# One burst of four attention-value groups, a ring of six probability tiles, and a stack load that is issued one step later

## What is computed

```
xn = layernorm(x)
q, k, v = xn @ Wq.T + bq, xn @ Wk.T + bk, xn @ Wv.T + bv      # 16 heads of 8
attn = softmax(where(causal, q @ k.T / sqrt(8), -inf))
a = (attn @ v) @ Wo.T + bo
top_val, top_idx = top_k(xn @ gate_w.T, 2);  w = softmax(top_val)
f = sum over the two of (xn @ We[top_idx]) * w
out = x + a + f
```

## Time and profile before

| | |
|---|---|
| median of three runs | 515.52 us (513.57 to 517.12) |
| the profiled execution | 512.65 us |
| its span, from first to last instruction | 510.5 us |
| TensorE matmul busy | 94% of the span |
| VectorE, ScalarE, GpSimd busy | 82%, 78%, 68% |
| mean granted clock of TensorE | 0.998 |
| DMA queue of SyncE | 66.68 MB, 53% of 16 engines |

### The profile page before, as it was taken

How to read it: one execution, slowest core, us unless ns; L and a number is a source line. 1 busy time by engine, 2 the same in 40 slices (tenths; PEclk the granted TensorE clock), 3 DMA queues, 4 the chain that set the end, 5 groups by cost and what they waited for, 6 DMA issues and landing times.

```text
span 510.5 us, 17312 instructions
## 1 busy us (share of the span) xinstructions
PE 477.8 (94%) x6274; PEld 393.8 (77%) x6274; DVE 420.7 (82%) x1111; ACT 396.9 (78%) x1062; POOL 345.9 (68%) x561
## 2 busy tenths in 40 slices
PE   2548799999999999999999999999999999999995
PEld 1437688888888888888888888888888888888863
DVE  5897698888888898888888898888888898888721
ACT  3644688888888888888888888888888888887773
POOL 7264657777777777778777777777777777755443
PEclk9999999999999999999999999999999999999999
DMA  4664746656547566655465566655556566552000
GB/s 124 195 140 117 188 122 152 161 136 156 134 119 162 130 151 156 160 139 145 105 168 128 148 154 160 156 141 143 139 128 147 138 152 161 133 132 44 15 13 22
DMA packets 64281, 67.79 MB, mean 133 GB/s; under 512 B 6828, under 2 KB 59180, under 8 KB 59484
## 3 DMA queue, kind: packets, MB, share of 16 engines
q1 hardware_dynamic: 64196, 66.68, 53.0%
HBM read 44.90 MB, written 21.23 MB: 130 GB/s over the span
## 4 chain that ended last, share of the span: by engine, by line
PE 89%; DVE 3%; ACT 3%; DMA 2%; issue 2%; SPq 0%; POOL 0%; DVEq 0%; POOLq 0%; ACTq 0%
PE m L841 23%; PE oT_ps L911 17%; PE scoreT_ps L887 13%; PE score_ps L867 12%; PE scoreT_ps L892 5%; PE score_ps L861 5%; PE m L953 3%; PE m L996 3%; PE m L1014 3%; PE m L926 2%; PE m L1021 1%; PE m L962 1%; DMA qstack<-mT 1%; ACT probs L499 1%; DVE negmax L625 1%
## 5 line engine op out<-in xcount | busy, mean ns | idle before, releaser
L625 DVE TENSOR_REDUCE negmax<-score_ps 128x2 f32<-128x512 f32 (+1 forms) x384 | 249.7, 678 | 46.4 <-PE score_ps L867 43.7
L499 ACT ACTIVATE probs<-scoreT_ps 128x512 f32<-128x512 f32 x384 | 216.5, 603 | 74.2 <-PE scoreT_ps L887 48.0
L394 POOL TENSOR_TENSOR fours<-lower,upper 128x512 f32<-128x512 f32 x64 | 81.7, 1276 | 54.1 <-ACT upper L549 54.1
L841 PE MATMUL m<-we_hl,xnT_hl 128*128 128x512 f32 x384 | 114.6, 420 | 0.0
L867 PE MATMUL score_ps<-kstack,qstack 72*128 72x128 bf16 (+1 forms) x1024 | 103.8, 224 | 5.6 <-DVE negmax L625 5.5
L887 PE MATMUL scoreT_ps<-qstack,kstack 123*128 123x128 bf16 (+1 forms) x1024 | 102.0, 221 | 3.3 <-DMA qstack<-mT 2.6
L911 PE MATMUL oT_ps<-probs,vaug 128*32 128x256 f32 (+1 forms) x2048 | 96.7, 329 | 0.2 <-ACT probs L499 0.2
L887 PEld LDWEIGHTS scoreT_ps<-qstack,kstack 123*128 123x128 bf16 (+1 forms) x1024 | 68.1, 98 | 26.5 <-ACT probs L499 15.4
L911 PEld LDWEIGHTS oT_ps<-probs,vaug 128*32 128x32 f32 x2048 | 57.3, 109 | 29.1 <-ACT probs L499 0.4
L549 ACT ACTIVATE upper<-m,weight 128x128 f32<-128x128 f32 x256 | 73.1, 376 | 8.2 <-PE m L841 8.2
L867 PEld LDWEIGHTS score_ps<-kstack,qstack 72*128 72x128 bf16 (+1 forms) x1024 | 72.1, 100 | 8.8 <-DVE negmax L625 7.6
(11 more groups left out here) (81 smaller groups left out, 649.7 us busy)
## 6 DMA issues: line engine op xcount, KB each, us to landing
kstack<-scratch SPq DMA_DIRECT2D x93, 192.0 KB
scratch<-parts SPq DMA_DIRECT2D x64, 192.0 KB, 2.4
qstack<-scratch SPq DMA_DIRECT2D x62, 192.0 KB
qstack<-scratch SPq DMA_DIRECT2D x31, 256.0 KB
x_sb<-in_x SPq DMA_DIRECT2D x32, 128.0 KB, 2.3
scratch<-parts SPq DMA_DIRECT2D x32, 128.0 KB, 1.9
out<-out_sb SPq DMA_DIRECT2D x32, 128.0 KB, 3.7
qstack<-mT SPq DMA_DIRECT2D x64, 8.0 KB, 2.1
```

What stands on the lines that cost most here:

```text
L394: g.tensor_tensor(fours[:, :, q, :], lower[:, :, q, :], upper[:, :, q, :], ALU.add).then_inc(pool_sum, 1)
L499: a.activation(o, i, ACT.Exp, scale=SCALE).then_inc(act_exp, 1)
L625: v.tensor_reduce(o, score_ps[n % 2][:].rearrange("p (h k) -> p h k", h=w), axis=AX.X, op=ALU.max, negate=True).then_inc(dve_max, 1)
L841: ins = tn.matmul(o, l, r, start=first, stop=l is low)
```

## The change

There are two edits. The first puts all four groups of `values` at place 6; groups 0 and 1 stood at place 3. Since more groups of exponentials are now alive at once, `probs` has six tiles that are taken in turn in place of four that are tied to the group, and ScalarE's wait for a free tile counts groups over all sequences. The second edit takes the load of the stacks of sequence 3 out of slot 1, where it was the last thing on SyncE's list, into slot 2, behind the two `mT` DMAs of sequence 1.

```diff
+PR = 6
-        probs = sbs("probs", [P, 3, HG, P], n=NG)
+        probs = sbs("probs", [P, 3, HG, P], n=PR)
@@ SyncE, slot
-                if s == 1:
-                    load_stacks(Seq(0, PRE), slice(0, H), dma_stack[PRE])
+                if 0 < s <= NB - PRE:
+                    load_stacks(Seq(0, s + 1), slice(0, H), dma_stack[s + 1])
...
                     store_parts(new)
-                    if s > 0:
+                    if s > NB - PRE - 1:
                         load_stacks(new, slice(0, H), dma_stack[new.buf])
@@ ScalarE, take_exp
-                pr = probs[grp]
+                pr = probs[(f.n * NG + grp) % PR]
...
-                    act.wait_ge(pe_pv, upto(f + (-1), per=NG, k=grp + 1))
+                    act.wait_ge(pe_pv, max(0, f.n * NG + grp + 1 - PR))
@@ TensorE, slot
-                    if n == 3 and has(s, -2):
-                        values(fin, 0)
-                        values(fin, 1)
...
                     if n == 6 and has(s, -2):
-                        values(fin, 2)
-                        values(fin, 3)
+                        for grp in range(NG):
+                            values(fin, grp)
```

More of the change, by code:

```diff
@@ L902, in values @@
                     pe.wait_ge(act_oT, upto(f + (-1)))
-                pr, va = probs[grp], vaug[f.buf]
+                pr, va = probs[(f.n * NG + grp) % PR], vaug[f.buf]
                 c0 = S * (grp // VGRP)
```

## The result

The changed kernel takes 530.13 us (median of 4 runs, 528.72 to 531.18), the kernel before 515.99 in the same comparison: a ratio of 1.0283, with a 95% interval of 1.0252 to 1.0314. The forecast was 527.0 us in a range of 517 to 533. The profiled execution has a span of 526.6 us, before 510.5, at a mean granted clock of 0.999.

The account below looks back on a forecast made before the run. The prediction took TensorE's list of matmuls to bound every steady slot. Lost cover +10.6, late rows +1.4, last slots -1.2 and second edit +0.7 gave +11.5 on 515.5, so 527.0 us, range 517 to 533.

Parts of the forecast that it names:

- TensorE's list is the bound, the others' distance from it must be read place by place: Steady slots: each takes the time of TensorE's matmul list, 14.39 us; busy totals hide how far behind other engines are.
- The joint: Each slot with `fin`: one of two values bursts goes, saving its cost beside its work, -0.23 us if nothing else changes.
- The lost cover: Place 4, second three expert products: without place 3's burst TensorE stands still 0.61 us; full slots get 0.38 us longer.
- `take_rest` as the link that ends last: Place 4: VectorE's `take_rest`, after ScalarE's `part1`, ends the expert products' wait; 0.25 to 0.6 us per slot, chance 0.72.
- Slots 30 to 32: Last slots, without a projection: -0.23 us each, perhaps -0.5 in the last, -1.2 us in all.
- Late maxima's rows: Item 0 of `scoreT_item`: TensorE asks for the `mT` rows sooner after their issue; 0.05 us a slot, +1.4 us in all.
- a wait of 3.3 us in slot 3 in place of 2.56 in slot 2: Second edit: TensorE's wait for the `mT` rows moves from slot 2 to slot 3; +0.7 us, bounds -2.6 and +1.5.
- The sum: Whole kernel: +10.6 + 1.4 - 1.2 + 0.7 = +11.5 us, giving a median of 527.0 us, 2.2% slower.

Follow-up runs that it names:

- the moved expert products: Changed kernel with the first of the two expert products of place 4 moved to place 3; 530.43 us, ratio 1.0308.
- the shorter exponential: Changed kernel with the exponential of item 8 taken for one head of four from sequence 2 on; 525.66 us.
- changed, `take_rest` first: Changed kernel with VectorE's take_rest ahead of the moments and the best experts at place 2, nothing else; 531.23 us.
- changed, both of these: Changed kernel with item 8's exponential for one head of four and take_rest first at place 2 of VectorE's list; 524.94 us.
- changed, one group stays: Changed kernel with group 0 of the values back at place 3, groups 1 to 3 at place 6; 515.94 us, ratio 1.0022.
- before, short exponential: Kernel before with the exponential of item 8 taken for one head of four from sequence 2 on; 515.07 us, ratio 0.9996.

## Why the prediction was right, point by point

- **TensorE's list is the bound, the others' distance from it must be read place by place.** Right.
- **The joint: -0.23 us.** Two bursts of 1.44 us with 0.31 us ahead of each took 3.50 us. One of 2.74 with 0.31, and the plain step of 0.23 us where the other burst stood, take 3.28. So 0.22 us was saved. Right.
- **The lost cover: 0.61 us.** The stops add up to 0.68 (0.16 + 0.16 + 0.36); the expert products started 0.12 us after `take_rest`, not 0.05. Net 0.44 a slot for 0.38, and 11.4 us for 26 slots.
- **`take_rest` as the link that ends last.** Right for the full slots; the moved expert products bared the wait, and the shorter exponential shortened it. That VectorE's own list was only some 0.15 us behind ScalarE's I had not seen.
- **Slots 30 to 32: -0.23 each, -1.2 in all.** Wrong, by sign: slots 30 and 31 lost 0.48 each and what follows 0.5. I had looked only at `take_rest`, which they don't have. The waits for the pairs, item 10 for the exponential of item 8 and item 4 for the maxima of item 2, hide inside 0.61 us in a full slot, but here they are the whole loss, as the timeline of slot 31 shows:

```profile
490.38 0.40 PE L888 MATMUL scoreT_ps<-qstack,kstack 123*128 123x128 bf16 x4 [0.23 <-ACT probs L500]
490.93 0.41 PE L868 MATMUL score_ps<-kstack,qstack 72*128 72x128 bf16 x4 [0.15 <-DVE negmax L626]
```

- **Late maxima's rows: 0.05 us a slot, 1.4 in all.** 2.2 us, in three slots of 0.5 to 1.0 us rather than spread. The rows did land sooner than before: in slots 4 to 29 the second DMA took at most 2.1 us from its issue in 18 of 26, in 9 of 26 before. That the emptier queue is the reason, as the forecast supposed, is not shown.
- **The second edit: a wait of 3.3 us in slot 3 in place of 2.56 in slot 2.** 2.96 us; the load of sequence 4 started at 67.27 (forecast 67.9), the rows were issued at 70.69 (71.0) and landed 5.3 to 5.6 us after their issue (5.8). Right in place and size in the profiled execution. The +0.7 us for the edit as a whole is not shown by any run: alone it gave 1.0030 (1.0001 to 1.0059), and on top of the first edit the ratio went from 1.0338 to 1.0283, with intervals that overlap. No term stood for the clock, which fell in the profiled execution of the second edit alone.
- **The sum: +11.5 us.** +14.1 on the medians, +16.1 on the spans; the forecast was right in its mechanism and somewhat low in its size. Of the 4.6 us that are missing in the spans, 2.7 are the last slots' wrong sign, 1.7 the 0.06 us in each of 28 slots, 0.8 the late rows, less 0.6 at the start.

## What to carry to other kernels

An engine without idle time says that its list is the bound, not that work may be moved on it freely: before a stretch is moved, subtract it from the time at which each instruction behind it is reached, and compare this with the end of what that instruction waits for, including the waits that nothing ends now. Slack has a size (0.97 us here), and up to it cover is free, beyond it each tenth is paid in each turn of the loop. Where an order is changed for a few turns at the start, look at the turn in which the new order meets the old one.

## What was not expected of the hardware

TensorE's clock fell with some waits at the start and not with others. A wait of 2.96 us (after) left it at 1.00; one of 2.60 us, in the changed kernel with the short exponential, was followed by 0.50, just behind its end:

```profile
76.00:77.00 1.00, 0.97 (x16) 0.76 (x20) 0.32 (x1) 0.55 (x2) 1.00 (x2) 1.00 0.48 142
77.00:78.00 1.00, 1.00 (x20) 0.58 (x16) 1.00 (x3) 1.00 (x5) 0.57 (x1) 0.66 0.45 106
78.00:79.00 1.00, 1.00 (x20) 0.76 (x16) 0.04 (x1) 0.09 (x1) 0.72 (x4) 0.50 0.75 213
```

Ten of the twelve profiles have such a wait for the maxima's rows in slot 2 or 3. The last column is what the slot took beyond its period and the wait.

| profile | wait, us | lowest clock with or behind it | beyond, us |
|---|---|---|---|
| changed, `take_rest` first | 2.19 | 0.50 | 1.8 |
| before | 2.56 | 1.00 | 0.2 |
| changed, short exponential | 2.60 | 0.50 | 2.0 |
| changed, both of these | 2.83 | 0.50 | 2.2 |
| changed | 2.96 | 1.00 | 0.2 |
| changed, expert products at place 3 | 3.21 | 0.50 | 1.8 |
| changed, one group stays | 3.83 | 0.50 | 2.8 |
| before, short exponential | 3.97 | 0.50 | 1.8 |
| first edit alone | 4.11 | 0.50 | 2.6 |
| second edit alone | 5.32 | 0.50 | 2.3 |

The length of the wait does not tell the falls apart, and the two profiles on which the forecast rests and is held against are the two without one. Of these ten, the six that show 0.50 also from about 29 to 43 us all fell again, and of the other four two did. What decides stays open. A fall costs 1.8 to 2.8 us here.

The clock column has to be held against the steps. In the kernel before it reads 1.00 from 21 to 47 us, yet items stand 0.43 to 0.44 us apart there, where they stand 0.23 apart later:

```profile
46.00:47.00 1.00, 1.00 (x9) 0.79 (x9) 0.09 (x1) 0.00 (x0) 0.76 (x2) 1.00 0.84 197
```

```profile
46.66 0.63 PE L887 MATMUL scoreT_ps<-qstack,kstack 123*128 123x128 bf16 x4
47.09 0.63 PE L861 MATMUL score_ps<-kstack,qstack 123*128 123x128 bf16 x4
```

Eight of the profiles show 0.50 from about 29 to 43 us, and items stand as far apart there (0.44 us, 42.05 to 42.49, in the changed kernel with the short exponential); in the other four that stretch reads 1.00. So a mean granted clock of 0.98 in one execution and 0.998 in another does not show that the first ran slower by as much.
